# Loads of a count matrix in a graph network kernel, issued from ScalarE's DMA queue instead of SyncE's

## What is computed

```python
h = relu(layernorm(x)); x = x + spline_block(h)         # 2 passes over the edges
h = relu(layernorm(x)); x = x + segment_sum(norm * h[src], dst)     # sum pass "gcn"
h = relu(layernorm(x)); x = x + mlp_block(h)            # 1 pass
h = relu(layernorm(x))
for l in range(3):                                      # 3 sum passes "mp"
    m = concatenate([h[dst], h[src], e], 1) @ W[l].T + b[l]
    h = relu(segment_sum(m, dst))
    if l < 2: h = relu(batchnorm(h))
x = x + h
```

## Time and profile before

| | us |
|---|---|
| median of 3 runs (lowest, highest) | 12152.77 (12142.07, 12161.24) |
| the profiled execution, its own time | 12167.19 |
| its span | 12165.4 |
| busy PE | 7389.9 |
| busy POOL | 8427.2 |
| busy ACT | 1294.4 |
| queue q1 (SP's transfers) | 1320.40 MB, 30.2% of 16 engines |
| queue q10 (ACT's transfers) | 181.80 MB, 4.9% |
| queue q0 (POOL's gathers and scatters) | 687.96 MB, 20.4% |

### The profile page before, as it was taken

One profiled execution on the slowest core, in us unless ns is written; L12 is line 12 of the kernel. 1 busy time (PEld: TensorE's weight loads), 2 busy tenths in 40 slices (PEclk: granted clock), 3 DMA queues, 4 the chain that ended last, 5 costly groups with the idle time before them and its releaser, 6 DMA issues. The chain is left out here.

```text
span 12165.4 us, 164494 instructions
## 1 busy us (share of the span) xinstructions
PE 7389.9 (61%) x47130; PEld 6315.5 (52%) x47130; DVE 5229.8 (43%) x11174; ACT 1294.4 (11%) x2960; POOL 8427.2 (69%) x8843
## 2 busy tenths in 40 slices
PE   4566666656556554111167756666666876876877
PEld 2444444434444443111167655555556866875866
DVE  6445555543555555666623234444442323223222
ACT  3201111110000000000000011111110000000000
POOL 0377777757777775666677767777776775775776
PEclk9888888877777776555588877777778988987988
DMA  7646666666666663000077744444446766865865
GB/s 290 257 140 202 191 204 196 195 205 198 205 211 216 204 220 100 1 1 1 17 260 264 233 123 120 121 121 122 121 121 232 266 222 214 279 221 182 314 228 195
DMA packets 916399, 2193.41 MB, mean 180 GB/s; under 512 B 309997, under 2 KB 523470, under 8 KB 802974
## 3 DMA queue, kind: packets, MB, share of 16 engines
q1 hardware_dynamic: 413950, 1320.40, 30.2%
q0 software_dynamic: 336000, 687.96, 20.4%
q10 hardware_dynamic: 166176, 181.80, 4.9%
HBM read 1644.03 MB, written 545.35 MB: 180 GB/s over the span
## 5 line engine op out<-in xcount | busy, mean ns | idle before, releaser
L843 POOL DMA_INDIRECT BIG<-t_cell,IDX x3330 | 3159.0, 949 | 1547.7 <-issue 1538.6
L1026 PE MATMUL PS<-BIG,OH 128*128 128x273 f32 (+3 forms) x12870 | 3155.2, 403 | 1353.3 <-DVE BIG L1843 984.0
L1026 PEld LDWEIGHTS PS<-BIG,OH 128*128 128x128 f32 (+1 forms) x12870 | 2442.6, 219 | 1930.8 <-issue 1435.4
L843 POOL DMA_INDIRECT BIG<-t_mp,IDX x2160 | 2053.1, 951 | 877.6 <-issue 865.4
L1115 PE MATMUL PS<-BIG 128*128 128x192 bf16 x22572 | 2227.4, 261 | 75.9 <-DMA BIG<-counts 73.8
L1115 PEld LDWEIGHTS PS<-BIG 128*128 128x128 bf16 x22572 | 2105.1, 104 | 124.7 <-issue 93.2
L843 POOL DMA_INDIRECT BIG<-t_p,IDX x1665 | 1597.2, 959 | 556.6 <-issue 555.4
L1843 DVE TENSOR_TENSOR BIG<-BIG,PS 128x1280 f32<-128x1280 f32 x666 | 989.2, 1485 | 1506.4 <-DMA BIG<-t_cell,IDX 1505.7
L1820 DVE TENSOR_TENSOR OH<-REL,PS 128x640 f32<-128x640 f32 (+1 forms) x1575 | 1268.9, 813 | 103.7 <-PE PS L1026 26.5
L825 POOL DMA_INDIRECT counts<-BIG x960 | 932.2, 971 | 492.7 <-issue 273.3
L1060 PE MATMUL PS<-BIG 128*128 128x128 f32 x3330 | 632.5, 356 | 800.8 <-DVE BIG L1850 792.6
(11 more groups left out here) (215 smaller groups left out, 5599.2 us busy)
## 6 DMA issues: line engine op xcount, KB each, us to landing
BIG<-counts SPq DMA_DIRECT2D x684, 1056.0 KB
t_cell<-BIG SPq DMA_DIRECT2D x198, 1280.0 KB, 5.3
counts<-BIG SPq DMA_DIRECT2D x37, 4884.0 KB
BIG<-in_dst_row ACTq DMA_DIRECT2D x333, 240.0 KB, 3.3
BIG<-t_cell,IDX POOLq DMA_INDIRECT x3330
BIG<-t_mp,IDX POOLq DMA_INDIRECT x2160
BIG<-in_ef ACTq DMA_DIRECT2D x333, 80.0 KB
BIG<-t_p,IDX POOLq DMA_INDIRECT x1665
```

The costliest lines, as they stand in the source:

```text
L843: nc.gpsimd.indirect_dma_start(to[:, j, :], None, table, bass.IndirectOffsetOnAxis(ap=IDX[:, at, column:column + 1], axis=0)).then_inc(gat ...
L1026: last = nc.tensor.matmul(WIN[:, 0:out_w], hot[:, j * P:(j + 1) * P], src[:, j, :], start=False, stop=(c == CHUNKS - 1 and j == CT - 1))
```

## The change

SP no longer loads the pieces. ACT does: its `load_third` stands in `next_thirds(u, s)`, which ACT runs at the end of each slot, behind `stage_window`, `store_window` and the node stages of that slot. The first three pieces are issued by ACT at the start of the pass, after the six index copies; in pass 2 behind a wait on the scattered counts (as SP did), in passes 5 and 6 behind a wait on all three parts of `HS` in SBUF (`normed`). In pass 4 there is no wait ahead of them. SP keeps the node stages' loads and stores, the store and load of `HS` and `phase_done`.

```diff
             def sum_pass(n):
                 kind, table, width, acc = passes[n]
-                gb, i = first_group[n], sum_passes.index(n)
...
-                def load_third(q, b):
-                    sp.dma_start(CB[b], thirds_of[bass.ds(q, 1)].rearrange("q p c -> (q p) c")).then_inc(third_in[b], 16)
-
-                def body(u, s):
-
-                    for x, q in enumerate(thirds_at(u, s)):
-                        b = (2 * s + x) % THIRDS if len(thirds_at(u, s)) == 2 else s % THIRDS
-                        if isinstance(q, int) and q + THIRDS >= z.thirds:
-                            continue
-                        sp.wait_ge(third_done, z.thirds * i + q + 1)
-                        hold(sp)
-                        load_third(q + THIRDS, b)
+                gb = first_group[n]
...
-                if n == 2:
-                    for h in range(2):
-                        sp.wait_ge(counts_out[h], 16 * TILES * (z.build_groups // 2))
-                        hold(sp)
-                for b in range(THIRDS):
-                    load_third(b, b)
...
+                sum_units(sp, lambda u, s: None, node)
...
             def sum_pass(n):
+                i = sum_passes.index(n)
...
+                def load_third(q, b):
+                    act.dma_start(CB[b], thirds_of[bass.ds(q, 1)].rearrange("q p c -> (q p) c")).then_inc(third_in[b], 16)
+
+                def next_thirds(u, s):
+
+                    for x, q in enumerate(thirds_at(u, s)):
...
+                        act.wait_ge(third_done, z.thirds * i + q + 1)
+                        hold(act)
+                        load_third(q + THIRDS, b)
...
                         if not is_step(u, 0):
                             sum_steps(node, u, s)
+                        next_thirds(u, s)
...
                 for g in range(RING):
                     copy_list(n, g, g)
+                if n == 2:
+                    for h in range(2):
+                        act.wait_ge(counts_out[h], 16 * TILES * (z.build_groups // 2))
+                        hold(act)
+                if n in (5, 6):
+                    act.wait_ge(sem(f"n{n}_normed"), PARTS)
+                    hold(act)
+                for b in range(THIRDS):
+                    load_third(b, b)
```

More of the change, by code:

```diff
@@ L706, in sum_pass @@
                 kind, table, width, acc = passes[n]
-                gb, i = first_group[n], sum_passes.index(n)
-                thirds_of = counts[0:z.thirds * P * z.third * P, :].rearrange("(q p c) o -> q p (c o)", p=P, c=z.third * P)
-                def load_third(q, b):
-                    sp.dma_start(CB[b], thirds_of[bass.ds(q, 1)].rearrange("q p c -> (q p) c")).then_inc(third_in[b], 16)
-                def body(u, s):
-                    for x, q in enumerate(thirds_at(u, s)):
-                        b = (2 * s + x) % THIRDS if len(thirds_at(u, s)) == 2 else s % THIRDS
-                        if isinstance(q, int) and q + THIRDS >= z.thirds:
-                            continue
-                        sp.wait_ge(third_done, z.thirds * i + q + 1)
-                        hold(sp)
-                        load_third(q + THIRDS, b)
+                gb = first_group[n]
                 def node(s, o, k, half):
@@ L1375, in sum_pass @@
             def sum_pass(n):
+                i = sum_passes.index(n)
+                thirds_of = counts[0:z.thirds * P * z.third * P, :].rearrange("(q p c) o -> q p (c o)", p=P, c=z.third * P)
+                def load_third(q, b):
+                    act.dma_start(CB[b], thirds_of[bass.ds(q, 1)].rearrange("q p c -> (q p) c")).then_inc(third_in[b], 16)
+                def next_thirds(u, s):
+                    for x, q in enumerate(thirds_at(u, s)):
+                        b = (2 * s + x) % THIRDS if len(thirds_at(u, s)) == 2 else s % THIRDS
+                        if isinstance(q, int) and q + THIRDS >= z.thirds:
+                            continue
+                        act.wait_ge(third_done, z.thirds * i + q + 1)
+                        hold(act)
+                        load_third(q + THIRDS, b)
                 def unit(u, h, left, node):
```

## The result

The changed kernel takes 12188.88 us (median of 11 runs, 12174.42 to 12219.78), beside 12156.22 us for the kernel before (median of 11 runs made with them, 12142.07 to 12161.89). The ratio is 1.0029, 95% interval 1.0021 to 1.0038: slower by 33 us. The forecast was 12191. The profiled execution took 12199.06 us, 31.9 more than the one before.

The account below looks back on a forecast made before the run. POOL's 720 gathers at 1.25 us set a sum pass; PE's delays cost only beyond a lead of 45 gathers. Held loads 9 + 8, starts 16 + 5 gave +38 on 12152.8, or 12191 us; range 12158 to 12220.

Parts of the forecast that it names:

- First loads of passes 5 and 6: Starts of passes 5 and 6: ACT's three loads delay the last `HS` store by 8 us each, +16 in all.
- First loads of pass 4: Start of pass 4: SP's last table store meets ACT's three pieces and lands later, +5 us.
- the bound of 6: Start of pass 4: the last table store would land up to 6 us later, never below 0.
- Held loads in pass 4: Loads behind node stages in pass 4: 12 us, less 2.5 of slack and 1.7 at the first piece, +8.
- as a sign: Profile sign: PE waits 3 to 4 us for `counts` behind slots 2 and 6 (3 and 7 in pass 2).
- the slack of 2.5 us: Pass 4: POOL 43 gathers ahead of PE, limit 45, so 2.5 us of PE delay would cost nothing.
- Held loads in passes 5 and 6: Loads behind node stages in passes 5 and 6: 12 us of delay against 16 of slack, 0.
- Held loads in pass 2: Loads behind node stages in pass 2: 12 us in slots 3 and 7, -3 in slots 4 and 8, +9.
- rival 3: Sum passes: PE falls back further, each held slot costs 6 us; +74 in all, 12227 us; chance 0.11.
- Rival 1: Only held loads cost, the `HS` store keeps its pace; +17 to +22, 12170 to 12175 us; chance 0.16.
- rival 2: The queue makes no difference, late issues are absorbed and POOL's waits could go; 12136 to 12153 us; chance 0.13.

Follow-up runs that it names:

- e1: Changed kernel, but ahead of passes 5 and 6 ACT waits for `phase_done` before its first three loads; 12149.72 us, ratio 1.0011.
- e7: Kernel before, with only the first three loads of each sum pass moved from SP to ACT; 12160.24 us, ratio 1.0020.
- e3: Changed kernel, but ahead of passes 5 and 6 one load goes beside the last `HS` store and two wait for `phase_done`; 12152.85 us.
- e4: Changed kernel with ACT's loads ahead of each slot's node stages instead of behind them; 12154.1 us, ratio 1.0016.
- e2: Changed kernel, but ahead of pass 4 too ACT waits for `phase_done` before its first three loads; 12188.62 us.
- e10: Kernel before, unchanged, run again for scatter; 12141.97 us.
- e9: Kernel before, but in slots 4 and 8 of pass 2 SP, still held, issues the pieces ahead of its two stores; 12131.3 us.
- e12: The same kernel as e9, timed against the kernel before; 12134.45 us, ratio 1.0002.
- e8: Changed kernel, loads ahead of node stages; first loads wait for `phase_done` (passes 5, 6) or the landing of `HS` (pass 4); 12138.9 us, ratio 1.0001.

## Why the prediction was right, and where it wasn't

The time was right, 12191 against 12188.9, by a sum whose terms were not all right. The mechanisms at the starts and of the held loads in passes 4 to 6 were as forecast; that the total came out within 3 us is in part luck, for errors of opposite sign met in it.

- *First loads of passes 5 and 6:* forecast +8 each, measured +7.9 and +9.5 in the profiled executions; over the seven traces that keep this order the time from the last gather to the first is 93.0 and 93.6 us on average, against 85.3 and 86.6 in the four that have SP's (+7.7 and +7.0). Shown by e1, e7 and the dose in e3. The Trainium skill's page "DMA: Bandwidth & Descriptors", section "Queues, rings and completion order", lets an engine change queues by the packet. By that rule, as the prediction worked it out, the store bears all of the loads' time, an estimate of 8.7 us from the earlier trace rows; 8.2 were measured on the store (15.8 less 7.6).
- *First loads of pass 4:* forecast +5, measured +6.3, and 6.7 over eight traces (58.1 against 51.4). Near the bound of 6, slightly beyond it. The table store itself landed 9.4 us after its issue, and 2.7 before.
- *Held loads in pass 4:* forecast +8, measured +9.3 in the profiled pair. The pass scatters: 901 to 908 us in five traces with SP's loads (mean 904.0), 905 to 912 in six with the changed order (mean 908.7), so +5 is the better figure, and the pair showed the upper end. The mechanism was right: issues 3.6 to 5 us late (4.6 forecast), PE waits of 2.11, 1.91, 1.69 and 3.53 us (3 forecast, and 3 to 4 as a sign), and e4's 902 us. Two sizes were off and partly cancelled. Over the same traces the 28th chunk came 5.8 us later (231.6 against 225.8 us) and not 12, and the slack of 2.5 us was read from the trace with the earliest 28th chunk of the five (222.3 us); on average there was none.
- *Held loads in passes 5 and 6:* forecast 0 by slack, measured nothing, with the 28th chunk 7 to 8 us later and still below 225. Right.
- *Held loads in pass 2:* forecast +9, measured -0.5 in the profiled pair, and about +1 on average over the traces (903.2 us in the changed kernel, e1, e2 and e3, 902.2 in the kernel before, e7 and e10). This is the step that failed. I gave slots 3 and 7 12 us and took 3 off for slots 4 and 8, where "ACT itself makes the copies that SP waited for, and issues at once": a credit for the issue alone. The table says +9 for slots 3 and 7 (10.0 less 1.0) and -11 for slots 4 and 8 (9.7 less 20.9). The credit was nearly four times too small, for two reasons. ACT issues not behind its last copy but while the first one runs, 1.6 us after the products begin where SP came at 3.4: 1.8 us sooner, not 0.7 to 0.9. And the piece no longer stands behind SP's two stores, which the prediction named and priced at nothing. By e9 and e12 the stores are 5 to 8 of the 11 us, and ACT's earlier issue the other 3 to 6. The four waits of slots 3 and 7 were 2.1 to 2.9 us each, so that the 12 was too much as well. The table doesn't close the account, though: by it pass 2 would be 2 us quicker to its 28th chunk, and over the same traces it was 3.8 us slower (226.1 against 222.3). Most of that stayed unpaid, since in two of the three traces with SP's order pass 2 had 4 to 5 us of slack; the forecast had read none from the third.

The total was forecast at +38 and is +33. Pass 2's missing 9.5 us are met by 4 us more at the starts of passes 4 and 6 and in pass 4 in the profiled pair, and the median of the kernel before in the 11 runs lies 3.4 us above the one that the forecast stood on.

One sum of the prediction is wrong: rival 3 has 6 us each for passes 5 and 6, where 24 less a slack of 16 is 8, so its time would be 12231 and not 12227. The forecast doesn't use it.

Rival 1 fell with the store's landing of 15.8 us, rival 2 with e1, e4 and e7, and rival 3 with passes 5 and 6. Rival 2 is nearly true of e8, though: once each load waits for what it waited for on SP, the queue makes no difference. The Trainium skill's page "DMA: Bandwidth & Descriptors", section "Issuing engines are not separate DMA queues", says that transfers of all issuers interleave on the same 16 engines; the traces agree, and 24 of the 33 us are that interleaving (e7), where one queue had kept the store and the load of `HS` ahead of the pieces.

The timed kernels fit this: 24 us for the starts alone (e7), 15 without those of passes 5 and 6 (e1), 19 without the held loads (e4), 3 without either (e8), each within some 12 us.

## What to carry to other kernels

A queue is also an order: before loads move to another engine's queue, list what stood behind what on the old one, and which of it gates other engines. Three prefetches of 1 MB beside the last store on which a pass waits cost this kernel 24 us over three passes, since the store bore nearly the full time of what moved beside it; all the loads held behind other stages cost only some 9 to 14 net. A load placed behind a wait on its engine cost here only what went beyond the lead of the engine that sets the end (some 14 of 38 us); so measure that lead stage by stage.

## What the runs showed of the hardware

- A store of 1584 KB in rows of 384 bytes, which lands in 7.6 us alone, lands in 10.9 to 11.1 with one transfer of 1056 KB in rows of 8448 bytes beside it on another queue (e3) and in 15.6 to 15.9 with three (fourteen stores in seven traces), so that it bore nearly all of their time.
- A store of 144 KB, which lands in 2.6 to 2.8 us alone, lands in 9.2 to 9.5 with the three pieces issued 1.3 to 2.1 us ahead of it on another queue.
- A load of `HS` (24.4 to 24.7 us from issue to first use) took 33.4 with the same three pieces beside it: also 8.7 to 9 us more.
- ACT took up a DMA issue at 6249.97, 0.09 us after the first of the four copies ahead of it in its program had begun and 0.9 us before the last one ended. The issue had no wait on these copies.
